# First stage of an attention kernel: chunks written out, one norm moved ahead, bias distances in the first chunk, first maxima among the last products

## What is computed

```
xn = layernorm(x)                                  # no gain
q, k, v = split(xn @ W_qkv.T)                      # 16 heads of 16
a = softmax(q @ k.T * 0.25 + bias)                 # 2048 x 2048 for each head and batch
s = (a @ v) @ W_proj.T + b_proj + layernorm(xn) * gamma + beta
g = silu(ffn(xn))                                  # 2 layers: local attention, windows of 128, and gated MLP
out = x + s * g
```

## Time and profile before

| | us |
|---|---|
| median of 3 runs | 2985.59 (2984.51 to 2985.92) |
| profiled execution | 2984.49 |
| its span, first to last instruction | 2982.7 |
| PE busy | 2937.4 (98%) |
| DVE busy | 2253.1 (76%) |
| ACT busy | 2300.1 (77%) |
| POOL busy | 1110.2 (37%) |

### The profile page before, as it was taken

The page is one execution under the profiler, slowest core; times in us unless marked ns, Lnnn a source line. Parts: engine busy times, 40 slices in busy tenths (PEclk is TensorE's granted clock), DMA queues, the critical chain, the costliest instruction groups (busy, mean ns, idle before and its releaser), DMA issues.

```text
span 2982.7 us, 97191 instructions
## 1 busy us (share of the span) xinstructions
PE 2937.4 (98%) x38016; PEld 1979.2 (66%) x38016; DVE 2253.1 (76%) x4091; ACT 2300.1 (77%) x4635; POOL 1110.2 (37%) x1835
## 2 busy tenths in 40 slices
PE   8899999999999999999989999999999999999998
PEld 4455555555555555555567777777777777777776
DVE  8888888888888888888756666666666666666664
ACT  4599999999999999999956666666666666666664
POOL 5321112122211221222155545555455555555554
PEclk9899999999999999999999999999999999999999
DMA  7631111111111111111011101111101111111110
GB/s 230 209 115 38 49 48 49 38 48 48 48 38 48 48 48 38 48 48 48 32 59 45 42 26 34 30 44 42 33 27 33 41 42 33 31 35 34 44 40 5
DMA packets 157207, 152.15 MB, mean 51 GB/s; under 512 B 17794, under 2 KB 130946, under 8 KB 156930
## 3 DMA queue, kind: packets, MB, share of 16 engines
q1 hardware_dynamic: 156930, 148.15, 15.8%
HBM read 89.37 MB, written 58.72 MB: 50 GB/s over the span
## 4 chain that ended last, share of the span: by engine, by line
PE 89%; DVE 8%; issue 2%; ACT 1%; SPq 0%; DVEq 0%; DMA 0%; POOL 0%; POOLq 0%; ACTq 0%
PE banks L1468 15%; PE banks L1430 15%; PE banks L1485 15%; PE banks L1535 8%; PE banks L1671 7%; PE banks L1684 6%; PE banks L1624 4%; PE banks L1636 4%; PE banks L1546 4%; PE banks L1585 3%; DVE masked L1247 3%; PE banks L1601 3%; PE banks L1557 1%; DVE heads_win L1323 1%; PE banks L1611 1%
## 5 line engine op out<-in xcount | busy, mean ns | idle before, releaser
L1140 DVE TENSOR_REDUCE pair_max<-banks 128x1 f32<-128x1024 f32 x1024 | 1219.7, 1222 | 145.9 <-PE banks L1430 116.1
L915 ACT ACTIVATE probs<-banks 128x512 f32<-128x512 f32 x2048 | 1158.7, 598 | 64.9 <-PE banks L1468 5.1
L1468 PE MATMUL banks<-q_aug,k_aug 98*32 98x512 bf16 x8192 | 1144.1, 381 | 0.8 <-ACT probs L915 0.4
L1430 PE MATMUL banks<-k_aug,q_aug 96*32 96x512 bf16 x8192 | 819.4, 382 | 5.6 <-ACT v_all L882 3.3
L1485 PE MATMUL banks<-probs,v_cur 128*32 128x256 f32 x8192 | 796.8, 379 | 0.2
L1468 PEld LDWEIGHTS banks<-q_aug,k_aug 98*32 98x32 bf16 x8192 | 391.8, 95 | 197.8 <-ACT probs L915 5.7
L1485 PEld LDWEIGHTS banks<-probs,v_cur 128*32 128x32 f32 x8192 | 366.6, 111 | 166.7 <-ACT acc_sb L896 0.7
L644 POOL TENSOR_SCALAR row_max<-pair_max 128x1 f32<-128x1 f32 x508 | 132.0, 283 | 887.6 <-DVE pair_max L1140 887.6
L1430 PEld LDWEIGHTS banks<-k_aug,q_aug 96*32 96x32 bf16 x8192 | 310.0, 97 | 218.2 <-DVE pair_max L1140 11.2
L1671 PE MATMUL banks<-hnT,w_sb 128*128 128x128 f32 (+1 forms) x2816 | 347.3, 280 | 3.6 <-ACT hnT L991 0.9
L1671 PEld LDWEIGHTS banks<-hnT,w_sb 128*128 128x128 f32 (+1 forms) x2816 | 324.8, 190 | 38.2 <-ACT hnT L991 25.1
(11 more groups left out here) (144 smaller groups left out, 3950.6 us busy)
## 6 DMA issues: line engine op xcount, KB each, us to landing
acc_scratch<-acc_sb SPq DMA_DIRECT2D x128, 256.0 KB, 2.4
heads_win<-acc_scratch SPq DMA_DIRECT2D x512, 64.0 KB
q_aug<-q_parts SPq DMA_DIRECT2D x192, 64.0 KB, 2.2
k_aug<-k_parts SPq DMA_DIRECT2D x192, 64.0 KB, 2.2
q_parts<-parts SPq DMA_DIRECT2D x16, 384.0 KB, 3.1
k_parts<-parts SPq DMA_DIRECT2D x16, 384.0 KB, 4.0
x_in<-in_x SPq DMA_DIRECT2D x10, 512.0 KB, 4.7
xT_scratch<-xnT SPq DMA_DIRECT2D x8, 512.0 KB, 5.1
```

What stands on the lines that cost most here:

```text
L915: nc.scalar.activation(probs[:, step % PRING, :], banks[:, ring(h, use), :], ACT.Exp, scale=SCALE).then_inc(prob_ready, 1)
L1140: nc.vector.tensor_reduce(pair_max[:, group % 2, q, half:half + 1], banks[:, 4 + 2 * (t % 2):6 + 2 * (t % 2), :], AX.XY, ALU.max).then_inc ...
L1430: last = nc.tensor.matmul(banks[m:m + CT, 4 + t % 4, :], q_aug[0:TERM_ROWS, b, q * P + m:q * P + m + CT], k_aug[0:TERM_ROWS, b, kq * BANK: ...
L1468: last = nc.tensor.matmul(banks[m:m + CT, ring(h, use), :], k_aug[0:AUG, b, kb * P + m:kb * P + m + CT], q_aug[0:AUG, b, qc * CHUNK:(qc + ...
```

## The change

The first stage's chunks are all written out. Norm of chunk 2 and residual of chunk 0 stand ahead of the loop. TensorE begins with 24 transposes of the identity. SP issues the loads of the centers before it waits for the first norms. The distances are made in chunk 0, reduced by POOL after chunk 1, scaled in chunk 6, and ScalarE's exponential of them stands in chunk 6. SP issues the first `load_aug` at the start of chunk 6's stores. The first six pairs of head 0 use banks 0 and 1 and stand between the products of chunk 7, so that 9 instead of 13 pairs stand before the first step; steps 0 to 7 have a pair each. ScalarE's wait for `phase1_end` stands behind the first shift.

```diff
+EARLY = 6
+WARM = 24
+FIRST_PAIRS = LEAD - 2 * (EARLY + 3)
...
+            for c in range(NCHUNK):
+                yield c, c // 2, c % 2, c < NCHUNK - 1, c < NCHUNK - 2
+
+        def pair_banks(h, pair):
+            return (0, 1) if h == 0 and pair < EARLY else (4 + 2 * (pair % 2), 5 + 2 * (pair % 2))
+
+        def pair_at(h, step):
+            if h == 0 and step < FIRST_PAIRS:
+                return EARLY + 3 + step
+            return (step + LEAD) // 2 if step % 2 == 1 else None
...
 # SP
+                if c == NCHUNK - 2:
+                    for mb in range(NMB):
+                        sp.wait_ge(parts_stored[mb], 16 * (NCHUNK // B + 1))
+                    load_aug(0, 0)
...
-                if ahead2:
+                if c + 4 < NCHUNK:
                     sp.wait_ge(xn_ready, c + 3)
-                    sp.dma_start(x_in[:, u], xv[bass.ds(after_next, 1)][0]).then_inc(x_loaded[u], 16)
-                elif ahead:
-                    for mb in range(NMB):
-                        sp.wait_ge(parts_stored[mb], 16 * (NCHUNK - 1))
-                    load_aug(0, 0)
+                    load(c + 4, u)
...
 # POOL
-                if not ahead2 and not ahead:
+                if c == 1:
                     pool.wait_ge(dist_red, 1)
                     nc.gpsimd.partition_all_reduce(dmax[:, 1:2], dmax[:, 0:1], P, RMAX).then_inc(dist_red, 1)
...
 # ScalarE
+            root(2, 0)
...
-                if ahead2:
+                if c == 0:
+                    act.wait_ge(dist_step, 5)
+                    nc.scalar.activation(dist[:], dist[:], ACT.Sqrt).then_inc(dist_sqrt, 1)
+                elif ahead2:
                     root(c + 2, u)
                 second_part(c, 3)
+                if c == NCHUNK - 2:
+                    act.wait_ge(dist_scale, 1)
+                    nc.scalar.activation(bias_exp[:], dist[:], ACT.Exp, scale=dmax[:, 4:5]).then_inc(dist_exp, 1)
...
 # VectorE, ahead of the chunks
+            dve.wait_ge(x_loaded[0], 32)
+            norm_stats(2, 0)
+            norm_variance(2, 0)
             dve.wait_ge(consts_in, 16 * NCONST)
+            residual(0, 0)
+            norm_apply(2, 0)
+            nc.vector.sem_inc(smax_read, 2)
...
 # VectorE, in the chunks
                 split_rest(c, 0)
+                if c == NCHUNK - 1:
+                    max_pair(0, 0)
+                elif c > 0:
+                    residual(c, u)
+                if c == 0:
                     dve.wait_ge(dist_in, 16 * 5)
...
+                split_rest(c, 1)
+                if c == NCHUNK - 1:
+                    max_pair(0, 1)
+                    residual(c, u)
...
+                elif ahead2:
+                    dve.wait_ge(x_loaded[u], it * 16 + 32)
+                    norm_stats(c + 2, u)
+                split_rest(c, 2)
+                if c == NCHUNK - 1:
+                    max_pair(0, 2)
+                if c > 0 and ahead2:
+                    norm_variance(c + 2, u)
+                split_rest(c, 3)
+                if c == 0:
+                    dve.wait_ge(dist_sqrt, 1)
+                    nc.vector.tensor_reduce(dmax[:, 0:1], dist[:], AX.XY, ALU.max).then_inc(dist_red, 1)
+                elif ahead2:
+                    dve.wait_ge(xT_done, c + 1)
+                    norm_apply(c + 2, u)
+                if c == NCHUNK - 2:
+                    scale_distances()
...
 # TensorE
             pe.wait_ge(pool_const, 2)
+            for _w in range(WARM):
+                nc.tensor.transpose(banks[:, 7, 0:P], ident[:], ident[:])
...
+                for mb in range(NMB):
+                    if mb == 2 and ahead:
+                        transpose_x(c + 1, 1 - u)
+                    project_qk(c, u, mb)
+                    if not ahead:
+                        if mb == 0:
+                            pe.wait_ge(aug_loaded[0], AUG_LOADS)
+                        max_pair(0, mb)
...
+                    if not ahead and j == 1:
+                        max_pair(0, NMB)
                 last.then_inc(v_done, 1)
+            max_pair(0, NMB + 1)
             pe.wait_ge(rest_ready, NMB * (NCHUNK + 1))
+            max_pair(0, EARLY)
             pe.wait_ge(v_saved, NCHUNK + 1)
...
+            max_pair(0, EARLY + 1)
...
             shift_rows(0, 0, 0)
-            for t in range(KB, LEAD):
-                max_tile(0, t)
+            max_pair(0, EARLY + 2)
```

More of the change, by code:

```diff
@@ L370, in items, with chunks @@
                 yield NWIN - 1, k, k < ITEMS - 1
[L371 to L377, removed]
+        def chunks():
+            for c in range(NCHUNK):
[6 more added lines that the diff above has]
+            return (step + LEAD) // 2 if step % 2 == 1 else None
         def ring(h, use):
@@ L423, in _ @@
             sp.dma_start(ccol[:, 2, :], centers[PTS - 1, :].partition_broadcast(P)).then_inc(dist_in, 16)
+            for c in range(2):
+                sp.wait_ge(xn_ready, c + 1)
+                load(c + 2, c)
             for u in range(2):
@@ L438, in load_aug @@
                                          ).then_inc(aug_loaded[b], 16)
-            for c, it, u, ahead, ahead2 in chunks(nc.sync):
-                if ahead2:
[L442 to L445, removed]
+            for c, it, u, ahead, ahead2 in chunks():
+                token = c * CHUNK
+                if c == NCHUNK - 2:
+                    for mb in range(NMB):
+                        sp.wait_ge(parts_stored[mb], 16 * (NCHUNK // B + 1))
+                    load_aug(0, 0)
                 rows = [(q_dram if mb < 2 else k_dram)[mb % 2 * (P // HD):(mb % 2 + 1) * (P // HD), :, :,
@@ L608, in _ @@
             nc.gpsimd.tensor_tensor(beta_sb[:], beta_sb[:], bproj_sb[:], ALU.add).then_inc(res_step, 1)
-            for c, it, u, ahead, ahead2 in chunks(nc.gpsimd):
+            for c, it, u, ahead, ahead2 in chunks():
                 for mb in range(NMB):
@@ L861, in _ @@
             root(1, 1)
-            for c, it, u, ahead, ahead2 in chunks(nc.scalar):
+            root(2, 0)
+            for c, it, u, ahead, ahead2 in chunks():
                 first_part(c, 0)
@@ L1172, in _ @@
                 for step in steps:
-                    tile = step + LEAD
-                    if ends and tile >= STEPS:
-                        continue
-                    if tile % 2 == 1:
-                        max_pair(h, tile // 2)
+                    pair = pair_at(h, step)
+                    if pair is not None and not (ends and pair >= PAIRS):
+                        max_pair(h, pair)
             dve.wait_ge(smax_read, HEADS * PAIRS + 2)
@@ L1401, in project_qk, with max_pair @@
                 last.then_inc(qk_done, 1)
+            def max_pair(h, pair):
+                b = pair // (PAIRS // B) % B
+                if h == 0 and pair < EARLY:
+                    pe.wait_ge(smax_read, pair + 2)
+                else:
+                    pe.wait_ge(smax_read, h * PAIRS + (pair + 1))
+                for half in range(2):
+                    t = 2 * pair + half
+                    q, kq = (t // (N // BANK)) % KB, t % (N // BANK)
+                    for m in range(0, P, CT):
+                        last = nc.tensor.matmul(banks[m:m + CT, pair_banks(h, pair)[half], :],
+                                                q_aug[0:TERM_ROWS, b, q * P + m:q * P + m + CT],
+                                                k_aug[0:TERM_ROWS, b, kq * BANK:(kq + 1) * BANK],
+                                                start=True, stop=True)
+                last.then_inc(smax_ready, 1)
             transpose_x(0, 0)
@@ L1507, in _ @@
                         weighted(h, group + ago, first, half)
-                    pair = (step + LEAD) // 2
-                    if step % 2 == 1 and not (ends and pair >= PAIRS):
+                    pair = pair_at(h, step)
+                    if pair is not None and not (ends and pair >= PAIRS):
                         if pair == PAIRS // 2:
```

123 lines of the change are left out of this document (39 added, 84 removed).

## The result

The changed kernel takes 2993.01 us (median of 13 runs, 2991.23 to 2995.32), against 2986.01 of before in the same comparison; ratio 1.0023, 95% interval 1.0016 to 1.003. It is 7.0 us slower, where I forecast 1.9 us faster, and lies above my range.

A forecast was written before the change was run, and what follows sets the result against it. TensorE and VectorE, both saturated, were taken to bound the first stage. Start +1.2, all-reduce +2.3 and end -5.4 gave -1.9 us from 2985.6: 2983.7 us, range 2978.5 to 2988.5.

The forecast's parts named there:

- the all-reduce's price: POOL after chunk 1: 6.1 us of POOL makes parts and stores late, VectorE idles; +2.3 us, bounds 0 and 2.9.
- Below nothing there is no way: Lower bound of the all-reduce's cost: it could be 0 but could not become a gain.
- the start: Up to chunk 1's split: first split at 20.1 to 20.9, chunk 1's split +1.2 us, bounds 0.5 to 2.1.
- E: Start of chunk 6's first split on VectorE, 88.83 us before; times of the end are distances from it.
- VectorE and TensorE are both full: Chunks after the all-reduce's delay: neither engine has slack, so nothing recovers and the +2.3 us stays.
- the end: From E to attention's step 8: 44.5 us before, shorter by 5.4 us, bounds -4.0 and -6.4.
- the lower of the two cases: TensorE's clock in attention's early steps: half speed, 1.3 us per step and pair, -5.0 us; otherwise -6.4.
- Writing the loop out: First stage's chunk loop: costs nothing, first chunk 11.44 us through the loop against 11.43 for repeated ones.
- Rival 3: SP's 12 loads before chunk 6's stores delay the first q store; end 7.2 us later, 2990.9 us; chance 0.12.
- Rival 4: All-reduce also locks VectorE in chunk 2, 2 us in addition, 2985.7 us; chance 0.10.
- Rival 1: All-reduce after chunk 1 is hidden and costs 0: -4.2 us, 2981.4 us; chance 0.25.
- rival 2: All-reduce hidden, clock at full speed, q stores in time, start +0.5: -7.2 us, 2978.4 us; chance 0.13.

The follow-up runs named there:

- experiment 1: Changed kernel with POOL's all-reduce replaced by a POOL copy: 2983.54 us, ratio 0.9991; with a second all-reduce right behind the first: 2996.25 us, one execution.
- experiment 2: Changed kernel with all-reduce back behind chunk 7's last POOL part, scale behind pair 8, distances' exponential behind the first shift: 2984.36 us, ratio 0.9991.
- experiment 3: Against experiment 2's kernel, distance products moved to chunk 6's end: 2983.32 us; then products behind chunk 0's last split, residual store earlier: 2980.72 us.
- experiment 4: Against e7_products_after_splits, one execution each: 16 transposes behind pair 7, 2986.49 us; phase1_end given before the second 12 loads, 2978.56 us.
- e12_no_warm: e7_products_after_splits without any warming transposes: 2979.64 us.
- e7_products_after_splits: Against experiment 2's kernel: distance products and sum behind chunk 0's last split, root and maximum in chunk 6, residual stores earlier: 2980.72 us, ratio 0.9978.
- e11_warm40_start: e7_products_after_splits with 40 instead of 24 warming transposes at the start: 3061.5 us (4 runs), ratio 1.0276.
- e8_all: e7_products_after_splits with 16 transposes at the shift, phase1_end earlier, chunk 2's input load before the centers' loads: 3079.53 us (5 runs), ratio 1.0307.

## Why the prediction was wrong

**Failed: the all-reduce's price, forecast 2.3 us (bounds 0 and 2.9), measured 9.7.** The mechanism was the forecast one: POOL's parts late, SP's stores late, and the engines that need them waiting. The size was wrong in three ways. First, I bounded the cost by the all-reduce's own row and took the 6.1 us up to its end as the whole; POOL was away for 13.1. The way back, 7.08 us, could not be seen before the change, because nothing that pays it was due. With a step that is moved, the instruction that follows it in the new place has to be priced as well, and here its kind changed from a copy to a tensor_tensor. Experiments 1 and 2 show this. Second, the stores of q were late enough to stop ScalarE (4.61 and 2.95 us), not only VectorE's residual (3.83 us). Third, TensorE waited 5.75 us for chunk 5's norm, made in the late chunk 3, and ran at half clock behind it (granted 0.50 from 77.2 to 80 us). Its wait of 4.25 us for chunk 3's norm is not part of this price: without the all-reduce it is 4.26. "Below nothing there is no way" held; the upper bound of 2.9 didn't. With 2.3 us here and the other two terms as measured (+2.5 and -4.9) the time would have stayed inside the range. A smaller fault is in the working: from 4.3 us late at the first part, POOL's 0.36 us of idle time before the addition gives 3.9 there and not 3.65, and the step to the store's 3.3 names no row. The Trainium skill (GPSIMD Engine Reference, "2.1 Instruction dispatch") gives about 6 us for the first call of a freshly loaded routine, with nothing visible in the profile. The traces show a gap of that size each time, 5.6 to 6.8 us; the way back is theirs alone.

**Partly right: the start.** Forecast: first split at 20.1 to 20.9, chunk 1's split +1.2 (0.5 to 2.1), and E later by the same. Measured 20.40 and +1.6, but +2.5 at E without the all-reduce (91.31 against 88.83), beyond 2.1 and inside the 3.1 that I had allowed for another reason, a late load. I let the delay run on unchanged. In fact chunk 2 took 1.4 us more, TensorE at its lower clock behind the wait for chunk 3's norm, and the three chunks after it gave back some 0.6 (11.2 us each). VectorE did idle 1.15 us for the load, which I had as a bound and took as 0; SP was held 4.8 us by the load of centers instead of 2.92. The six differences took 1.6 us and not 3.9: POOL's first part has its row from 21.81 on, among them, but here it is POOL's row that is long, 1.86 us. The second product took 3.11 us, beside POOL's addition of 3.07. I had left open whether the products wait; by the Trainium skill's rule cited there ("SBUF: two separate sides") they do, and the trace agrees: the addition ends at 26.71, the product 0.8 us later. That chunk 0 is ended by ScalarE's chain was right (0.83 and 0.95 us of VectorE idle). My step "VectorE and TensorE are both full" hid that the order could still win: experiment 3 has E 3.9 us earlier than experiment 2 with the same work in another order.

**Right in size: the end.** Forecast -5.4, measured -4.9. The shift was out at E + 28.5, forecast 28.3, with TensorE at full clock until then. The first exponential was released by phase1_end at E + 33.2 (forecast 32.5). Steps 0 to 6 ran at 1.28 us each at the lower clock (0.51 granted), the lower of the two cases that I had weighed. Three steps on the way were wrong: TensorE came to chunk 7 at E + 8.6 and not + 8.0; chunk 7's first part came at E + 10.5 and not + 11, and not released by SP's store but behind the exponential and its table load; and TensorE paced the steps from step 0 on, while I had let steps 3 to 7 follow the first exponential, which held them by 0.15 us at most (experiment 4). That the sum came out all the same is partly luck.

**Taken as constant:** all behind step 8. The feed-forward stage took 2.1 us more than before, which is inside what it does from one variant to the next; why is open.

**Writing the loop out** cost nothing that the first stage shows, as forecast. Its possible cost is one I hadn't thought of, the place of later loops. In the changed kernel it did not arise: no instruction packets in 1700 to 2600 us.

**Rivals.** Rival 3, SP's 12 loads, didn't happen: they took 5.7 us (101.41 to 107.11). Rival 4, a lock on VectorE, didn't either: while POOL stood from 44.3 to 49.9, VectorE's residual took 1.66 us, less than the 2.56 beside a working POOL. Rival 1 is the reverse of what happened, and rival 2 needed the same hidden all-reduce. No rival had POOL stand longer than the all-reduce's own row. The range was drawn narrower than its parts: their bounds add up to -5.9 and +2.0, not to 3 on either side of -1.9; the result lies outside both.

## What to carry to other kernels

A step moved into a full stage costs what stands before it, itself, and what its successor pays; look in the trace for a successor of the same kind, and where there is none, leave that end of the range open. A custom POOL instruction between ordinary ones belongs where POOL has 13 us to spare, or next to another of its kind. Making an engine faster ahead of a wait gains nothing and can cost its clock behind the wait. After a change ahead of a long loop, look at the instruction queue's packets inside that loop before believing a time: 16 transposes moved one here by 59 to 105 us.

## What the runs showed of the hardware

- POOL stands 5.6 to 6.8 us before an all-reduce over partitions and 7.0 to 7.8 us before the next tensor_tensor, over all the traces with one; a copy behind it runs at once (experiment 2), and so does a second all-reduce (experiment 1).
- In the first stage TensorE's clock was at its lower level (0.50 granted) behind its waits of 4.25, 4.26, 4.52 and 5.75 us for the norm of chunk 3 or 5, and at the upper one (1.00) behind those of 0.68 and 1.69 us (`e12_no_warm`, `e7_products_after_splits`). In attention's steps 3 to 7 the lower level cost 1.3 us (experiment 2).
- The loop of the feed-forward stage ran either without instruction packets in 1700 to 2600 us, or with 64 to 81 and then 59 to 105 us slower (`e11_warm40_start`, `e8_all`). 32 TensorE instructions more ahead of it turned one into the other, but not in every kernel that had them.
- A chunk of the first stage can go at 11.2 us: without the all-reduce the later chunks were 11.2 us apart (68.91, 80.11, 91.31) and not 11.43, VectorE's residual taking 1.66 us instead of 2.56 because POOL worked at another time, and TensorE busy 22.40 of 22.40 us. So the 11.43 us was VectorE's pace, though TensorE showed 57.02 of 57.10 us busy. This is argued from the rows; no run changed it alone.
